# GpSimd splits an expert's second weights in eight pieces instead of one

## The reference, cut to what matters

```
logits = xt @ wg ; top 2 of 8 experts, capacity 1024 tokens each
h = relu(disp[e] @ w1[e] + b1[e])      # 1024 x 256 @ 256 x 1024
y = h @ w2[e] + b2[e]                  # 1024 x 1024 @ 1024 x 256
out = x + attention(xn) + sum over the two experts of gate * y
```

## Time and profile before

| | |
|---|---|
| median of 3 runs | 804.64 us (800.29 to 807.0) |
| profiled execution | 808.55 us, span 806.8 us |
| busy share of the span | TensorE 88%, VectorE 65%, ScalarE 59%, GpSimd 52% |
| w2 copy, w2 subtraction on GpSimd | x8 each, 1898 and 4593 ns |
| split hl on VectorE | x128, 692 ns median, 4708 ns at most |

### The profile page before, as it was taken

One profiled execution on the slowest core, in us unless ns is written; L12 is line 12 of the kernel. 1 busy time (PEld: TensorE's weight loads), 2 busy tenths in 40 slices (PEclk: granted clock), 3 DMA queues, 4 the chain that ended last, 5 costly groups with the idle time before them and its releaser, 6 DMA issues. The chain is left out here.

```text
span 806.8 us, 18921 instructions
## 1 busy us (share of the span) xinstructions
PE 707.6 (88%) x5805; PEld 606.9 (75%) x5805; DVE 527.1 (65%) x1888; ACT 479.2 (59%) x1503; POOL 423.1 (52%) x714
## 2 busy tenths in 40 slices
PE   2643399999999999999999998999999799999976
PEld 2333279889798897979889797778787678778765
DVE  7699244453644526454453633889999879999994
ACT  2442075380834717355371733888999788998881
POOL 2555651340603315042340303889999879999992
PEclk9966589999999999999999997899999989999895
DMA  8460421231413214131231003021323223230311
GB/s 283 136 234 0 141 83 55 90 99 46 145 43 130 64 52 144 38 127 63 84 104 46 7 27 112 28 80 60 110 82 87 92 66 93 75 113 28 113 58 37
DMA packets 50941, 70.12 MB, mean 87 GB/s; under 512 B 4784, under 2 KB 43440, under 8 KB 50864
## 3 DMA queue, kind: packets, MB, share of 16 engines
q1 hardware_dynamic: 44368, 52.37, 20.0%
q0 software_dynamic: 6144, 16.79, 6.9%
q10 hardware_dynamic: 352, 0.04, 0.0%
HBM read 48.28 MB, written 16.78 MB: 81 GB/s over the span
## 5 line engine op out<-in xcount | busy, mean ns | idle before, releaser
L1021 ACT ACTIVATE a_p<-a_p,a_nmax 128x128 f32<-128x128 f32 x512 | 198.3, 392 | 34.3 <-DVE a_nmax L1051 33.4
L952 POOL TENSOR_SCALAR a_p<-a_p,a_rsum 128x128 f32<-128x128 f32 x512 | 199.0, 405 | 23.9 <-DVE a_rsum L1058 21.5
L692 DVE TENSOR_TENSOR m_hl<-m_hf,m_hh 128x512 fp32r<-128x512 f32 x128 | 114.7, 908 | 98.6 <-ACT m_hh L649 83.8
L55 PE MATMUL m_psY<-m_w2h,m_hh 128*128 128x256 f32 x512 | 145.0, 283 | 0.0
L55 PE MATMUL m_psY<-m_w2l,m_hh 128*128 128x256 f32 x512 | 143.9, 281 | 0.0
L55 PE MATMUL m_psY<-m_w2h,m_hl 128*128 128x256 f32 x512 | 143.8, 281 | 0.0
L645 ACT ACTIVATE m_hf<-m_psF,b1T 128x512 f32<-128x512 f32 x128 | 88.3, 690 | 88.0 <-PE m_psF L55 64.9
L1051 DVE CUSTOM_DVE_ANT_0 a_p<-a_psS,mask 128x128 f32<-128x128 f32 x512 | 116.5, 280 | 10.3 <-PE a_psS L1172 5.3
L55 PE MATMUL m_psF<-m_xh,w1h 128*128 128x512 f32 x256 | 103.5, 404 | 12.5 <-DVE m_hl L692 11.0
L613 POOL CAST m_w2h<-raw 128x2048 fp32r<-128x2048 f32 x8 | 15.2, 1898 | 185.6 <-PE m_psY L55 185.5
L55 PE MATMUL m_psF<-m_xl,w1h 128*128 128x512 f32 x256 | 101.6, 397 | 0.0
(11 more groups left out here) (188 smaller groups left out, 1392.9 us busy)
## 6 DMA issues: line engine op xcount, KB each, us to landing
raw<-in_L_ffn_w SPq DMA_DIRECT2D x16, 1024.0 KB, 5.2
y_scratch<-y SPq DMA_DIRECT2D x64, 128.0 KB, 1.7
n_xin<-in_L_attn_x SPq DMA_DIRECT2D x8, 512.0 KB, 7.7
xn_scratch<-n_xn SPq DMA_DIRECT2D x8, 512.0 KB, 2.9
xnr<-xn_scratch SPq DMA_DIRECT2D x8, 512.0 KB, 3.9
a_res<-in_L_attn_x SPq DMA_DIRECT2D x8, 512.0 KB, 3.5
out<-a_res SPq DMA_DIRECT2D x8, 512.0 KB
b2b<-in_L_ffn_b SPq DMA_DIRECT2D x8, 128.0 KB, 7.0
```

Source lines behind the costliest of these rows:

```text
L55: last = pe.matmul(out, a, b, start=(n_start and i == 0), stop=(n_stop and i == n - 1))
L692: dve.tensor_tensor(hl[:, u // HC, u % HC, :], hf[:, u % FR, :], hh[:, u // HC, u % HC, :].bitcast(fp32), ALU.subtract).then_inc(hl_done, 1)
L952: pool.tensor_scalar(e, e, rsum[:, r, j:j + 1], 0.0, ALU.mult, ALU.add).then_inc(norm_done, 1)
L1021: act.activation(e, e, ACT.Exp, scale=-1.0, bias=nmax[:, r, j:j + 1], accum_out=sums[:, r, j:j + 1]).then_inc(exp_done, 1)
```

## The change

`split_w2` goes over the HC = 8 chunks of 256 elements, a copy and a subtraction for each. Chunks 0, 1 and 2 follow each other at once; chunk c from 3 on waits until 2c - 4 splits hl of this expert are done (2, 4, 6, 8, 10). The semaphores w2h_done and w2l_done now go up by eight an expert, and the waits of SP and TensorE for them are adapted. Nothing else differs.

```
 @block.sync
-                    alone(sp, w2h_done, e + 1)
-                    alone(sp, w2l_done, e + 1)
+                    alone(sp, w2h_done, (e + 1) * HC)
+                    alone(sp, w2l_done, (e + 1) * HC)
                     sp.dma_start(raw2[:, :, :], w2v[:, bass.ds((e + 1) * HC, HC), :]).then_inc(raw2_in, 16)
 @block.gpsimd
                 alone(pool, raw2_in, (e + 1) * 16)
-                pool.tensor_copy(w2h[:, :, :], raw2[:, :, :]).then_inc(w2h_done, 1)
-                alone(pool, w2h_done, e + 1)
-                pool.tensor_tensor(w2l[:, :, :], raw2[:, :, :], w2h[:, :, :].bitcast(fp32), ALU.subtract)\
-                    .then_inc(w2l_done, 1)
+                for c in range(HC):
+                    if c > 2:
+
+                        alone(pool, hl_done, e * U + FR + 2 * c - 4)
+                    pool.tensor_copy(w2h[:, c, :], raw2[:, c, :]).then_inc(w2h_done, 1)
+                    alone(pool, w2h_done, e * HC + c + 1)
+                    pool.tensor_tensor(w2l[:, c, :], raw2[:, c, :], w2h[:, c, :].bitcast(fp32), ALU.subtract)\
+                        .then_inc(w2l_done, 1)
 @block.tensor
-                pe.wait_ge(w2h_done, e + 1)
-                pe.wait_ge(w2l_done, e + 1)
+                pe.wait_ge(w2h_done, (e + 1) * HC)
+                pe.wait_ge(w2l_done, (e + 1) * HC)
```

## The result

The changed kernel took 791.81 us in the median of four runs (789.64 to 797.2), the kernel before 805.82 in its four; a later set of 6 and 11 runs on one chip gave 792.54 (788.94 to 795.1) and 804.57 (800.81 to 809.33), ratio 0.9852 with a 95% interval of 0.9816 to 0.9888. So the change takes 12 us, 1.5%, off the time; 792.0 had been forecast.

The account below looks back on a forecast made before the run. TensorE was taken as the bound, with a 1.80 us first-layer hole in seven of eight experts; closing it gives 7 x 1.80 = 12.6 us with all else free, so 804.64 - 12.6 = 792.0 us, range 788.5 to 800.

Parts of the forecast that it names:

- What bounds the kernel, and the size of the hole: TensorE bounds each expert; its first layer's fifth unit waits for the first split, 1.80 us in seven experts, and this closes.
- The pieces: On GpSimd, each 256-element copy takes 0.40 us and each subtraction 0.74; with 0.18 between, 1.32 us a piece.
- hl(0) gets in after one short instruction: VectorE's first split waits for at most one GpSimd instruction, 0.81 us, and ends by 156.73, 1.4 us spare.
- xl, with one input in PSUM, would not be held up: VectorE's xl operation is not delayed beside a busy GpSimd; its kin in attention lasts 0.679 to 0.693 us: no term.
- The later pieces and the ninth unit: Pieces from 3 on don't pile up; ninth unit has 0.26 us spare: cost nothing, top 0.5 us an expert.
- Rival 1: At the ninth unit, part of the closed hole comes back: 8 x 0.5 = 4 us, time 796; chance 0.16.
- The queues: GpSimd's gathers and SP's w2 load move later; last piece has 4.8 us spare, fourth gather some 8: no cost.
- Rival 2: Something else holds the fifth unit near 159.9, or the last pieces come late: no change, 804.6 us; chance 0.09.
- rival 3: Units 2 to 11: VectorE and GpSimd alternate, VectorE falls behind; loss from 2.2 us hold, time 818 at 2.5; chance 0.07.
- The total: Whole kernel: 7 x 1.80 = 12.6 us less, nothing given back; median 804.64 to 792.0 us, -1.6%.
- One of the prediction's own signs of being wrong: Attention, which the diff leaves alone, taking other than 312 us by more than a few would show the prediction wrong.

Follow-up runs that it names:

- short subtractions twice: The changed kernel with each of its eight 256-element subtractions done twice; 823.34 us, ratio 1.0164 to the kernel before.
- long subtraction twice: The kernel before with its one long subtraction done twice in a row; 843.85 us against 808.1, ratio 1.044.
- late pieces: The changed kernel with its five paced pieces released three pairs of splits later (8 to 16); 857.29 us, ratio 1.0606 to the kernel before.

## Why the prediction was right

*What bounds the kernel, and the size of the hole.* Right. 1.80 us in seven experts was read off the starts of TensorE's rows, and a period became 1.83 shorter; the fifth unit was put at 158.10 and came at 158.09, the second layer at 175.43 and came at 175.39. Counting from the wait list alone, 1.57 an expert, would have given 11.0 us instead of 12.8.

*The pieces.* Right: 0.398 and 0.745 us in the median against 0.40 and 0.74 estimated. The subtractions get up to 1.26 long by waiting for a split, which was foreseen as harmless.

*hl(0) gets in after one short instruction.* Right, and shown from both sides: eight pieces without a break leave no split over 1.28 us, and two long subtractions in a row are parted by a split. That xl, with one input in PSUM, would not be held up is borne out too: 0.69 us at most in the changed kernel and with all pieces at once.

*The later pieces and the ninth unit.* Nothing is lost there: 164.20 - 158.09 = 6.11 us over four units, as in expert 0 before. Rival 1 did not happen in the changed kernel; its size, put at 0.5 us an expert, is 0.11 where the splits are 2.2 us late (the halves and the deeper ring).

*The queues.* The index copy came at 171.24 where the last piece was forecast to end at 170.6: the eighth subtraction waits for a split (1.25 us). The fourth gather starts at 176.03 (175.8 forecast). No wait comes of either. The w2 load is issued at 171.54.

*Rival 2* (no change) and *rival 3* (slower) did not happen. Rival 3's formula is wrong in kind as well. It lets VectorE fall behind when a piece holds GpSimd for long. With two subtractions a piece, VectorE still waited for at most one instruction at a time, and it was GpSimd that fell behind, to within 0.9 us of the second layer. The danger of more GpSimd work is at the last piece and behind it, not at the splits.

*The total.* 12.8 us by the periods, 12.0 by the medians, 12.6 forecast. The 18.7 us between the two profiles hold 5.9 us of attention, whose length follows the clock that the execution was granted. One of the prediction's own signs of being wrong came up: attention was to take 312 us but for a few, and took 306.8. The sign was badly chosen, since the prediction left the clock of attention out; the gain in the experts does not hang on it.

*What the prediction had not separated:* whether the pieces must be paced, and whether they must be eight. They need not. Two halves without a wait for the splits give the same time (791.81 against 792.54 us), and so does the old pair of instructions with a deeper ring (792.88). No version tried beats the changed kernel by more than the runs' spread. Within the experts there is hardly a hole left to close: from 152.14 to 480.00 us TensorE is busy for 327.3 of 327.9 us.

## To carry to other kernels

When an operation on a shared port delays another engine, compare the hold with the spare of the one who waits: here 4.6 us against 2.2, and anything that made the hold shorter than the spare, or the spare longer than the hold, gave the whole 12 us. Price such a hole by the starts of the bound engine's rows against a stretch of the same trace without it. And ask of every wait whether its semaphore says what is needed: TensorE needed a free bank and waited for a split of another buffer.

## What was not expected of the hardware

TensorE's clock after a hole. The 1.8 us hole of the kernel before leaves the granted clock at 1.00, that is 2.4 GHz. Most longer holes come with a stretch at the lower level, 1.2 GHz, behind them or from within them: the five of 2.1 to 2.8 us (short subtractions twice), five of the seven of 3.3 us (long subtraction twice), and seven of the eight of 3.7 to 3.8 (late pieces). In the one at 187.76, from 187 to 192 us, the granted clock is 0.50, the matmuls come 0.213 us apart, and a hole of 4.0 us by the starts costs 6.5. But experts 2 and 6 of the long subtraction twice and the last expert of the late pieces (3.7 us idle) stay at 1.00. So in these rows the length of a hole alone does not decide whether the clock falls; what does is not shown.

The Trainium skill (TensorE: Matmul & The Clock Gate, Part 1) has the array fall back to 1.2 GHz after it has stood idle, and matmuls then start N ÷ 1.2 GHz apart. For 256 columns that gives 213 ns, an estimate by that page; the rows of the late pieces agree, with 0.213 us.

VectorE held back until the gathers are issued. In the kernels with late pieces and with the short subtractions twice, VectorE's second bias row starts 1.50 to 1.60 us after the last of eight gathers is issued in 11 of 14 experts, up to 5 us after its input is ready, with nothing before it on its own queue. ScalarE shows the same distance in the kernel before (in expert 1 gathers issued until 174.83, hf of unit 13 at 176.40), where nobody waited for it, and no longer in the changed kernel. Neither late gathers nor late pieces alone bring it about. Two causes can be ruled out for expert 1 of the late pieces: a buffer of the row that had not been stored, since the last store of the expert before was issued at 161.39, and the loading of instructions, since the profile has no such packet between 152 and 260 us. What VectorE waits for is in no row, and stays open.
